# A four-layer decoder kernel: cross attention in row quarters and halves with a fourth buffer, one subtraction moved to GpSimd, and other counts of unread products at the norms

## The chip, the cores and the metric

The kernel runs on one core of a Trainium2 chip, as one program. The metric is device time in microseconds of one execution, lower is better. TensorE does the matrix products (the profile shows its weight loads apart, as PEld), VectorE (DVE), ScalarE (ACT) and GpSimd (POOL) the elementwise work, and SyncE (SP) issues the transfers. A matrix product reads a moving operand of up to 512 columns from SBUF, against weights loaded before, and writes to one of eight PSUM banks.

## The reference

Twelve stages run one after another over x, two sequences (B = 2) of 512 tokens of width 128: four layers of self attention, cross attention and feed forward. Each adds to x what it computes from a norm of x. The change is in two kinds of cross attention, and at the norms. Cut to those, in numpy's manner:

```
# l0x: 16 heads of 64, context of 77 rows of width 96 and one null key (78 keys), a key mask
q = norm(x) * g @ Wq ; k, v = context @ Wkv            # 16 heads of 64 columns
s = q_h @ k_h.T / 8, masked                            # (512, 78) per head and sequence
x = x + norm(concat_h(softmax(s) @ v_h) @ Wout) * g_out
# l2x, l3x ("narrow"): 16 heads of 8 inside a width of 128, 77 keys
q = norm(x) @ Wq + bq ; k = context @ Wk + bk ; v = context @ Wv + bv
s = q_h @ k_h.T / sqrt(8)                              # l2x: clipped to +-10000 before its softmax
x = x + concat_h(softmax(s) @ v_h) @ Wo + bo
```

## The kernel before

The program is written by hand: every engine has its own list of instructions, in the order in which the code below issues them, and the engines meet at counting semaphores (`then_inc` raises one, `wait_ge` waits for it). Nothing is scheduled or reordered by a planner; `plan` only gives the items of work their PSUM banks. x stays in SBUF throughout. The stages are called l0a, l0x, l0f, l1a, ... l3f (a self attention, x cross attention, f feed forward).

**A cross attention loop** is one of 16 steps. In l0x, l2x and l3x a step is eight heads (`half`) of one tile of 128 query tokens (`qt`, NQ = 4) of one sequence (`b`). A step's work goes round the engines:

- TensorE (`cross_tensor`): the scores of eight heads into two banks (`a.scores`), 128 x 616 or 128 x 624 numbers. At L816 two heads of 64 rows share one product of 128 rows, since `keys_own` holds zeros in the other head's rows; in the narrow stages (L1615) `keys_own` holds all 128 rows for each of the 16 heads, with a head's own eight rows kept and the others zero.
- VectorE (`cross_vector`): in l2x a clip from PSUM to SBUF (L709), then the maxima (L711), the subtraction of them (L712), and for the step before the sums of the exponentials (L717) and their reciprocals (L720).
- ScalarE (`cross_scalar`): the exponential (L731), and the copy of the turned probabilities of two steps back out of PSUM (L738).
- GpSimd (`cross_gpsimd`): the probabilities, exponentials times reciprocals (L748).
- TensorE again: eight transposes of the probabilities of step k - 2 (L686), and the values of step k - 6: two heads a step. In l0x (L827) they are of 64 columns each, and VectorE copies them out (L894). In the narrow stages (L1623) `values_own` holds for each head 128 columns, zero but for the head's own eight, and all sixteen heads add up in one bank, over 512 tokens at a time.

The probabilities `m.xp` have three buffers (k % 3), so the first instruction of VectorE's step k waits until step k - 3 is transposed.

**At every norm** VectorE takes moments of four tiles at a time (`half_moments`, L133 to L143, which raises `var_ready`), GpSimd the power -1/2 (L184), VectorE scales the tiles (L158), TensorE transposes them (L209) and ScalarE copies them out (L217). Meanwhile TensorE runs products of the identity whose result nobody reads (`keep_busy`, L193): `first` of them, then `second` after the second half's variance. `turned` waits for ScalarE's copies before the projections.

**At the start** `consts` are loaded in one queue by SyncE (L3026), and every other engine waits for all of them; among them are `rows8` and `cols8`, by which the narrow stages make `keys_own` (L1674) and `values_own` (L1712).

## Time and profile before

| | us |
|---|---|
| median of 3 runs | 1818.76 (1816.85 to 1821.48) |
| the profiled execution | 1830.47 |
| its span, first to last instruction | 1828.6 |
| TensorE busy in it | 1582.6 |
| VectorE busy | 1039.3 |
| ScalarE busy | 678.5 |
| GpSimd busy | 376.1 |
| mean granted TensorE clock | 0.907 of full |

The profiled execution is 11.7 us longer than the median of the others. Times in the rows below are of this one. "x8" in a row is a count of instructions; a matrix product of 32-bit numbers shows as two records (one product of 512 columns as x2), a transpose as one. `[0.78 <-PE psum L819]` is idle time of the engine before the row, and what ended it. A granted clock of 1.00 is 2.4 GHz, 0.50 is 1.2 GHz.

### The profile page before, as it was taken

Reading aid. Unit: us, or ns where it says so; the run is one execution under the profiler, and the core shown is the slowest. Engines: PE = TensorE matmul, PEld = TensorE weight load, DVE = VectorE, ACT = ScalarE, POOL = GpSimd, SP = SyncE. Lnnn points to the kernel's source line nnn. Section 1 sums busy time; section 2 is a strip of 40 time slices with the busy share of each in tenths; the row PEclk is TensorE's granted clock in tenths of the full one; section 3 lists DMA queues with packets and bytes.
Section 4 is the critical chain, followed back from the end, with each engine's and each line's share of the span. In section 5 each row is a group of like instructions: output and inputs, shape, how many; then the busy total and the mean of one; then the engine's idle time right before and its main releaser. Section 6 shows DMA issues by size and latency. Waiting matters only on the chain. (4 is left out here: it accounts for less than half of the span.)

```text
span 1828.6 us, 24507 instructions
## 1 busy us (share of the span) xinstructions
PE 1582.6 (87%) x9019; PEld 953.6 (52%) x9027; DVE 1039.3 (57%) x1963; ACT 678.5 (37%) x1652; POOL 376.1 (21%) x366
## 2 busy tenths in 40 slices
PE   6999899999999989968988848836989988899996
PEld 3665446445555565554567535522435555564444
DVE  4676574334554555567392366489875554465665
ACT  3774331333555534423102134213555555460001
POOL 3000120001000000033011034255764433410000
PEclk8999999998787889989687979977999999899999
DMA  3000002210000000000104000000111100100000
GB/s 128 2 2 4 1 1 102 97 46 13 1 1 1 1 14 8 9 3 0 60 1 156 9 29 39 20 15 24 35 35 18 18 13 14 17 7 24 23 23 12
DMA packets 14075, 46.92 MB, mean 26 GB/s; under 512 B 3032, under 2 KB 4870, under 8 KB 13328
## 3 DMA queue, kind: packets, MB, share of 16 engines
q1 hardware_dynamic: 13968, 45.49, 8.1%
q8 instruction: 68, 1.11, 0.3%
q14 instruction: 39, 0.32, 0.1%
HBM read 40.73 MB, written 0.56 MB: 23 GB/s over the span
## 5 line engine op out<-in xcount | busy, mean ns | idle before, releaser
L503 DVE TENSOR_REDUCE quad_max<-psum 128x1 f32<-128x128 f32 (+3 forms) x256 | 113.6, 486 | 116.2 <-PE psum L399 115.9
L184 POOL TENSOR_TENSOR rstd<-var,minus_half 128x4 f32<-128x4 f32 x30 | 30.6, 1022 | 655.2 <-DVE var L143 585.5
L468 ACT ACTIVATE pt<-psum,quad_max 128x128 f32<-128x128 f32 (+3 forms) x256 | 133.5, 525 | 83.0 <-DVE quad_max L503 80.5
L193 PE MATMUL psum<-ident 128*128 128x128 f32 x960 | 124.4, 293 | 45.0 <-DVE wide L2069 20.9
L2433 PE MATMUL psum<-slots,xn_t 128*128 128x512 f32 x256 | 113.8, 606 | 42.1 <-DVE pt L2606 42.1
L193 PEld LDWEIGHTS psum<-ident 128*128 128x128 f32 x960 | 120.6, 208 | 49.3 <-DVE wide L2069 21.5
L2469 PE MATMUL psum<-pt,slots 128*128 128x512 f32 x256 | 129.8, 594 | 2.1 <-DVE pt L2619 1.9
L2619 DVE TENSOR_TENSOR pt<-psum,wide 128x512 f32<-128x512 f32 x128 | 87.8, 691 | 52.9 <-PE psum L2462 43.8
L2303 DVE TENSOR_REDUCE duo_max<-psum 128x1 f32<-128x512 f32 x128 | 82.3, 686 | 56.4 <-PE psum L2204 55.3
L415 PE MATMUL psum<-ident,pt 128*128 128x128 f32 x640 | 99.9, 306 | 12.0 <-DVE wide L1212 10.8
L2433 PEld LDWEIGHTS psum<-slots,xn_t 128*128 128x128 f32 x256 | 48.1, 193 | 107.6 <-DVE pt L2606 52.6
L2278 ACT ACTIVATE p<-psum,duo_max 128x512 f32<-128x512 f32 x128 | 86.8, 683 | 46.7 <-DVE duo_max L2303 41.5
L2519 ACT ACTIVATE pt<-psum,p 128x64 f32<-128x64 f32 x256 | 58.0, 393 | 101.4 <-POOL wide L2673 51.0
L775 ACT ACTIVATE o_t<-psum 128x512 f32<-128x512 f32 x20 | 11.7, 595 | 216.4 <-PE psum L567 145.9
L415 PEld LDWEIGHTS psum<-ident,pt 128*128 128x128 f32 x640 | 81.7, 160 | 17.5 <-DVE wide L1212 12.3
L748 POOL TENSOR_TENSOR p<-p,xrsum 128x616 f32<-128x616 f32 (+1 forms) x48 | 58.6, 1222 | 146.3 <-DVE xrsum L720 146.3
L1090 DVE TENSOR_TENSOR p<-p,wide 128x512 f32<-128x512 f32 x64 | 44.1, 692 | 76.8 <-ACT p L1037 66.8
L2218 PE MATMUL psum<-ident,p 128*128 128x128 f32 x512 | 70.5, 279 | 18.9 <-DVE wide L2328 18.9
L2263 DVE COPY pt<-psum 128x512 f32<-128x512 f32 x64 | 44.2, 691 | 72.5 <-PE psum L2218 72.5
L686 PE MATMUL psum<-ident,p 128*77 128x128 f32 (+1 forms) x384 | 58.2, 300 | 29.5 <-POOL p L748 29.1
L2238 PEld LDWEIGHTS psum<-pt,wide 128*64 128x64 f32 x1024 | 58.2, 143 | 48.9 <-issue 20.0
L2204 PE MATMUL psum<-heads 64*128 64x512 f32 x256 | 75.5, 669 | 6.3 <-POOL heads L2350 6.3
(451 smaller groups left out, 3181.1 us busy)
## 6 DMA issues: line engine op xcount, KB each, us to landing
slots<-in_s_l2f SPq DMA_DIRECT2D x8, 578.0 KB, 3.8
keys_own<-in_s_l2f SPq DMA_DIRECT2D x8, 578.0 KB, 5.6
slots<-in_s_l0f SPq DMA_DIRECT2D x8, 514.0 KB, 3.6
wide<-scratch_gates SPq DMA_DIRECT2D x8, 512.0 KB, 7.6
slots<-in_s_l3v SPq DMA_DIRECT2D x8, 512.0 KB, 3.7
slots<-in_s_l3o SPq DMA_DIRECT2D x8, 512.0 KB, 3.6
weights<-in_w_l1a SPq DMA_DIRECT2D x1, 2624.0 KB, 9.1
weights<-in_w_l0x SPq DMA_DIRECT2D x1, 2113.0 KB, 10.7
```

The lines of the kernel that those rows point to most:

```text
L193: nc.tensor.matmul(m.ps[bank][:, 0:P], m.ident[:, :], m.ident[:, :], start=True, stop=True, skip_group_check=True)
L415: last = nc.tensor.transpose(bank[:, g * P:(g + 1) * P], m.quad_p[:, n % 2, g, kt * P:(kt + 1) * P], m.ident[:, :])
L468: nc.scalar.activation(m.quad_p[:, i % 2, g, 0:keys], m.ps[g][:, 0:keys], ACT.Exp, bias=m.quad_max[:, i % 2, g:g + 1], accum_out=sum_colum ...
L503: nc.vector.tensor_reduce(m.quad_max[:, n % 2, g:g + 1], m.ps[g][:, 0:keys], AX.X, ALU.max, negate=True).then_inc(m.quad_negmax, 1)
L748: nc.gpsimd.tensor_tensor(pr, pr, m.xrsum[:, k % 2, :].rearrange("p (h o) -> p h o", o=1).broadcast_to([P, 8, nk]), ALU.mult).then_inc(m.p ...
L2204: nc.tensor.matmul(m.ps[2 * (n % 2) + e], m.pair_rope[own, r % 2, 0, b * S + qt * P:b * S + (qt + 1) * P], m.pair_rope[own, r % 2, 1, b * ...
L2218: last = nc.tensor.transpose(bank[:, kt * P:(kt + 1) * P], m.p[:, 2 * (n % 2) + e, kt * P:(kt + 1) * P], m.ident[:, :])
L2278: nc.scalar.activation(m.p[:, 2 * (i % 2) + e, :], m.ps[2 * (i % 2) + e], ACT.Exp, bias=m.duo_max[:, i % 2, e:e + 1], accum_out=m.duo_sum[ ...
L2303: nc.vector.tensor_reduce(m.duo_max[:, n % 2, e:e + 1], m.ps[2 * (n % 2) + e], AX.X, ALU.max, negate=True).then_inc(m.duo_negmax, 1)
L2433: nc.tensor.matmul(m.ps[n % MIX_BANKS], m.xn_t[:, t * P:(t + 1) * P], m.slots[:, pair % 2, h * S:(h + 1) * S], start=True, stop=True).then ...
L2469: nc.tensor.matmul(m.ps[6 + b], m.slots[:, s, e * P:(e + 1) * P], m.gated[:, q % 4, :], start=False, stop=False, skip_group_check=True).th ...
L2619: tt(m.gated[:, k % 4, :], m.ps[k % 4], out, ALU.mult).then_inc(m.spread_gated, 1)
```

## The change

1. **Score products by rows.** In l0x each head's 64 rows are a product of their own (eight of 78 columns a step, even heads in one bank and odd ones in the other, in turn), and the mask's product comes first. In l2x and l3x `keys_own` has 32-row quarters: a product covers four heads on 32 rows, and a step has two such products, on two quarters, in two banks.
2. **Value products by columns in l2x and l3x.** A head's `values_own` has the 32 columns of its quarter; each product writes 32 partitions of the bank, for the 128 tokens of one tile. They come after every second step, 16 at a time; for that the steps go tile by tile with `half` innermost (`narrow_units`).
3. **Four buffers** for the probabilities, and the transposes of step k - 3 instead of k - 2 in TensorE's order.
4. **l2x:** VectorE keeps the clip and the maxima, GpSimd subtracts (L761 of the new file), and VectorE's sums are of step k - 2.
5. **l0x:** ScalarE copies the values out, and `context_v`; the norm stands first in VectorE's order.
6. **Unread products.** `busy_through_norm` has a third group, `turned` adds four in each of its 14 calls, other groups stand in the second and third step of a cross loop, two before the transposes of each narrow step.
7. **`rows8` and `cols8`** are no longer loaded.

The diff, cut to its core (other callers of `busy_through_norm` change their counts only: l0f 13, 16 to 12, 6, 12 and 12, 8 to 14, 6; l1f, l2a, l3a and the first of l3f 12, 8 to 12, 6; l2f 12, 8 to 12, 8, 10; the second of l3f 12, 16 to 14, 6, 10; where no third count stands it is 4):

```diff
-def busy_through_norm(nc, pe, m, norm, first, second):
+def busy_through_norm(nc, pe, m, norm, first, second, third=4):
+
     keep_busy(nc, m, first)
     pe.wait_ge(m.var_ready, 2 * norm)
     keep_busy(nc, m, second)
+    pe.wait_ge(m.rstd_ready, 2 * norm - 1)
+    keep_busy(nc, m, third)
...
-def turned(m, pe, name):
+def turned(nc, m, pe, name):
+    keep_busy(nc, m, 4)
...
-    for k in range(XSTEPS + 6):
+    for k in range(XSTEPS + 3 + NQ):
         if k < XSTEPS:
             b, half, qt = units[k]
             wait(pe, m.negmax_ready, a.s0 + k - 1)
-            for j in range(2):
-                last = a.scores(m.ps[2 * (k % 2) + j], b, half, j, qt)
-            last.then_inc(m.scores_ready, 1)
-        j = k - 2
+            a.scores([m.ps[2 * (k % 2) + e] for e in range(2)], b, half, qt).then_inc(m.scores_ready, 1)
+            if k in (1, 2):
+                keep_busy(nc, m, (14, 4)[k - 1], 7)
+        j = k - 3
...
-    for k in range(XSTEPS + 1):
+    lag = 2 if a.clip else 1
+    for k in range(XSTEPS + lag):
...
             if a.clip:
                 m.dve.done(nc.vector.tensor_scalar(to, scores, a.clip, -a.clip, ALU.min, ALU.max))
-                scores = to
-            m.dve.done(nc.vector.tensor_reduce(m.xmax[:, k % 2, :].rearrange("p (g h) -> p g h", g=2), scores, AX.X, ALU.max))
-            nc.vector.tensor_tensor(to, scores, spread(m.xmax[:, k % 2, :]), ALU.subtract).then_inc(m.negmax_ready, 1)
-        j = k - 1
+                wait(dve, m.negmax_ready, a.s0 + k - 1)
+                nc.vector.tensor_reduce(largest, to, AX.X, ALU.max).then_inc(m.xmax_ready, 1)
+            else:
+                m.dve.done(nc.vector.tensor_reduce(largest, scores, AX.X, ALU.max))
+                nc.vector.tensor_tensor(to, scores, spread(m.xmax[:, k % 2, :]), ALU.subtract).then_inc(m.negmax_ready, 1)
+        j = k - lag
...
-    for k in range(XSTEPS):
-        pool.wait_ge(m.rsum_ready, a.s0 + k + 1)
-        pr = m.xp[:, k % 3, 0:8 * nk].rearrange("p (h k) -> p h k", k=nk)
-        nc.gpsimd.tensor_tensor(pr, pr, m.xrsum[:, k % 2, :].rearrange("p (h o) -> p h o", o=1).broadcast_to([P, 8, nk]),
-                                ALU.mult).then_inc(m.probs_ready, 1)
+    heads = lambda k: m.xp[:, k % XP_BUFFERS, 0:8 * nk].rearrange("p (h k) -> p h k", k=nk)
+    each = lambda ap: ap.rearrange("p (h o) -> p h o", o=1).broadcast_to([P, 8, nk])
+    lag = 2 if a.clip else 0
+    for k in range(XSTEPS + lag):
+        if a.clip and k < XSTEPS:
+            pool.wait_ge(m.xmax_ready, k + 1)
+            nc.gpsimd.tensor_tensor(heads(k), heads(k), each(m.xmax[:, k % 2, :]), ALU.subtract).then_inc(m.negmax_ready, 1)
+        j = k - lag
+        if j >= 0:
+            pool.wait_ge(m.rsum_ready, a.s0 + j + 1)
+            nc.gpsimd.tensor_tensor(heads(j), heads(j), each(m.xrsum[:, j % 2, :]), ALU.mult).then_inc(m.probs_ready, 1)
...
+    def scores(banks, b, half, qt):
+        for e in range(2):
+            nc.tensor.matmul(banks[e][:, 0:4 * nk], m.ones_bf[0:1, :], m.mask_row[0:1, b, :], start=True, stop=False,
                              skip_group_check=True)
-        return nc.tensor.matmul(bank[:, 0:4 * nk], m.ones_bf[0:1, :], m.mask_row[0:1, b, :], start=False, stop=True,
-                                skip_group_check=True)
+        for i in range(4):
+            g = 4 * half + i
+            for e in range(2):
+                rows = slice(64 * e, 64 * e + 64)
+                last = nc.tensor.matmul(banks[e][:, i * nk:(i + 1) * nk], m.wide[rows, g, b * S + qt * P:b * S + (qt + 1) * P],
+                                        m.keys_own[rows, b, g * nk:(g + 1) * nk], start=False, stop=i == 3,
+                                        skip_group_check=True)
+        return last
...
+        units = narrow_units()
+        own = lambda g: slice(32 * g, 32 * g + 32)
+        for k in range(XSTEPS + 5):
+            if k < XSTEPS:
+                b, half, qt = units[k]
+                if clip:
+                    wait(pe, m.xmax_ready, k - 1)
+                else:
+                    wait(pe, m.negmax_ready, a.s0 + k - 1)
+                for x in range(2):
+                    rows = own(2 * half + x)
+                    last = nc.tensor.matmul(m.ps[2 * (k % 2) + x][:, 0:GROUP * SC], m.q_t[rows, b * S + qt * P:b * S + (qt + 1) * P],
+                                            m.keys_own[rows, b, 0:GROUP * SC], start=True, stop=True)
+                last.then_inc(m.scores_ready, 1)
+                if k in (1, 2):
+                    keep_busy(nc, m, (16, 4)[k - 1], 7)
+            n = k - 3
+            if 0 <= n < XSTEPS:
+                pe.wait_ge(m.probs_ready, a.s0 + n + 1)
+                wait(pe, m.cross_taken, a.x0 + n)
+                keep_busy(nc, m, 2, 4)
+                for h in range(8):
+                    last = nc.tensor.transpose(m.ps[4 + h // 4][0:SC, (h % 4) * P:(h % 4 + 1) * P],
+                                               m.xp[:, n % XP_BUFFERS, h * SC:(h + 1) * SC], m.ident[:, :])
+                last.then_inc(m.turned_ready, 1)
+            n = k - 5
+            if n >= 0 and n % 2 == 1:
+                b, _, qt = units[n]
+                pe.wait_ge(m.cross_taken, a.x0 + n + 1)
+                if n == 1:
+                    pe.wait_ge(m.narrow_values, a.v0 // 2 + 1)
+                bank = fill(m, pe, f"{stage}o{b}") if qt == 0 else m.ps[6 + b]
+                for j in range(GROUP):
+                    for g in range(GROUP):
+                        last = nc.tensor.matmul(bank[own(g), qt * P:(qt + 1) * P], m.values_own[0:SC, b, g, j, :],
+                                                m.xpt[0:SC, g // 2, g % 2 * GROUP + j, qt * P:(qt + 1) * P],
+                                                start=qt == 0 and j == 0, stop=qt == NQ - 1 and j == GROUP - 1,
+                                                skip_group_check=True)
+                last.then_inc(m.pv_done if qt < NQ - 1 else filled(m, f"{stage}o{b}"), 1)
```

**The order of TensorE in l0x**, in the second half of the loop, before: `keys_own,wide` are the scores, `mask_row,ones_bf` the mask, `ident,p` the transposes, `pt,context_v` the values.

```order
L827 MATMUL psum<-pt,context_v 64x512 x2
L816 MATMUL psum<-keys_own,wide 128x156 x2
L819 MATMUL psum<-mask_row,ones_bf 128x312
L816 MATMUL psum<-keys_own,wide 128x156 x2
L819 MATMUL psum<-mask_row,ones_bf 128x312
L686 MATMUL psum<-ident,p 78x128 x8
```

The same place after:

```order
L847 MATMUL psum<-pt,context_v 64x512 x2
L831 MATMUL psum<-mask_row,ones_bf 128x312 x2
L837 MATMUL psum<-keys_own,wide 128x78 x8
L691 MATMUL psum<-ident,p 78x128 x8
L847 MATMUL psum<-pt,context_v 64x512 x2
```

Two masks now stand together ahead of eight narrower score products; the transposes are those of the step before the ones they were.

**The order of TensorE at the end of l2x's loop**, before: `keys_own,q_t` are the scores, `pt,heads` the values.

```order
L1615 MATMUL psum<-keys_own,q_t 128x308 x2
L686 MATMUL psum<-ident,p 77x128 x8
L1623 MATMUL psum<-pt,heads 128x512 x2
L686 MATMUL psum<-ident,p 77x128 x8
L1623 MATMUL psum<-pt,heads 128x512 x2
L686 MATMUL psum<-ident,p 77x128 x8
L1623 MATMUL psum<-pt,heads 128x512 x10
```

After:

```order
L1643 MATMUL psum<-keys_own,q_t 128x308 x2
L193 MATMUL psum<-ident 128x128 x2
L1654 MATMUL psum<-ident,p 77x128 x8
L193 MATMUL psum<-ident 128x128 x2
L1654 MATMUL psum<-ident,p 77x128 x8
L1666 MATMUL psum<-pt,heads 32x128 x16
L193 MATMUL psum<-ident 128x128 x2
L1654 MATMUL psum<-ident,p 77x128 x8
L193 MATMUL psum<-ident 128x128 x2
L1654 MATMUL psum<-ident,p 77x128 x8
L1666 MATMUL psum<-pt,heads 32x128 x32
```

Fourteen value products of 512 columns stood behind the last scores' transposes; now 48 of 128 columns do, each of 32 columns of weights.

**The order of VectorE in l2x's loop**, one step, before and then after:

```order
L709 TENSOR_SCALAR p<-psum 128x616
L711 TENSOR_REDUCE xmax<-p 128x8
L712 TENSOR_TENSOR p<-p,xmax 128x616
L717 TENSOR_REDUCE xsum<-p 128x8
L720 RECIPROCAL xrsum<-xsum 128x8
```

```order
L716 TENSOR_SCALAR p<-psum 128x616
L718 TENSOR_REDUCE xmax<-p 128x8
L726 TENSOR_REDUCE xsum<-p 128x8
L729 RECIPROCAL xrsum<-xsum 128x8
L716 TENSOR_SCALAR p<-psum 128x616
```

The subtraction left VectorE, and the sums behind it belong to a step one earlier than they did.

## Rows read from the trace of the kernel before

**Rows 1.** The page's costliest groups: busy, mean ns of one, idle before.

```profile
L748 POOL TENSOR_TENSOR p<-p,xrsum 128x616 f32<-128x616 f32 (+1 forms) x48 | 58.6, 1222 | 146.3 <-DVE xrsum L720 146.3
```

**Rows 2.** Busy time by stretch: length, each engine's busy us, granted clock, DMA.

```profile
229.00:261.00 32.00, 31.75 (x178) 18.52 (x178) 24.68 (x41) 13.05 (x16) 9.84 (x8) 1.00 0.00 1
...
825.00:866.50 41.50, 35.99 (x155) 21.57 (x153) 31.22 (x49) 15.56 (x20) 10.95 (x9) 1.00 0.00 0
866.50:892.60 26.10, 24.77 (x45) 12.27 (x45) 1.67 (x4) 3.78 (x5) 2.44 (x2) 0.52 0.00 0
...
1105.30:1115.00 9.70, 6.49 (x22) 4.46 (x21) 6.50 (x11) 3.17 (x4) 6.32 (x3) 0.74 0.00 0
1115.00:1125.50 10.50, 7.60 (x41) 5.69 (x40) 8.99 (x15) 4.88 (x6) 3.65 (x3) 0.92 0.01 2
1125.50:1162.50 37.00, 35.70 (x153) 21.40 (x151) 23.30 (x39) 15.40 (x20) 10.95 (x9) 1.00 0.00 1
1162.50:1180.30 17.80, 15.76 (x41) 8.08 (x40) 0.99 (x3) 3.97 (x5) 2.39 (x2) 0.81 0.00 0
```

**Rows 3.** Timeline of one l0x step: start, us, instruction, idle before.

```profile
239.93 1.07 PE L686 MATMUL psum<-ident,p 128*78 128x128 f32 x8
...
240.93 1.08 PE L827 MATMUL psum<-pt,context_v 78*64 78x512 f32 x4
...
241.94 0.80 PE L816 MATMUL psum<-keys_own,wide 128*128 128x156 f32 x4
...
242.41 0.64 DVE L894 COPY wide<-psum 128x512 f32<-128x512 f32 x1
...
243.96 0.81 DVE L711 TENSOR_REDUCE xmax<-psum 128x8 f32<-128x624 f32 x1 [0.91 <-PE psum L819]
```

**Rows 4.** Timeline of two l2x steps.

```profile
841.88 1.10 PE L686 MATMUL psum<-ident,p 128*77 128x128 f32 x8 [1.16 <-POOL p L748]
842.42 0.80 DVE L712 TENSOR_TENSOR p<-p,xmax 128x616 f32<-128x616 f32 x1
...
842.82 1.88 PE L1623 MATMUL psum<-pt,heads 77*128 77x512 f32 x4
...
844.54 1.20 PE L1615 MATMUL psum<-keys_own,q_t 128*128 128x308 f32 x4
...
850.53 1.10 PE L686 MATMUL psum<-ident,p 128*77 128x128 f32 x8 [1.16 <-POOL p L748]
```

**Rows 5.** Timeline of the values behind the loops of l2x and l3x.

```profile
874.73 17.27 PE L1623 MATMUL psum<-pt,heads 77*128 77x512 f32 x20
...
1170.41 9.21 PE L1623 MATMUL psum<-pt,heads 77*128 77x512 f32 x20
```

**Rows 6.** Timeline of products on 32 rows or columns in l0a.

```profile
56.18 1.08 PE L430 MATMUL psum<-pt,wide 128*32 128x128 f32 x32
57.19 0.91 PE L397 MATMUL psum<-k_t,heads 32*128 32x384 f32 x4
58.03 0.28 PE L399 MATMUL psum<-future,ident_bf 128*128 128x128 bf16 x2
```

**Rows 7.** Timeline of weight loads on 32 rows (l0a) and 128 rows (l0x).

```profile
57.19 0.30 PEld L397 LDWEIGHTS psum<-k_t,heads 32*128 32x128 f32 x4 [0.20 <-issue]
...
201.84 0.56 PEld L816 LDWEIGHTS psum<-keys_own,wide 128*128 128x128 f32 x4
```

**Rows 8.** Timeline of the first step of l2x.

```profile
793.60 9.90 POOL L1712 TENSOR_TENSOR heads<-context_v,cols 77x2048 f32<-77x2048 f32 x2 [4.26 <-DVE context_v L1680]
...
801.33 2.82 DVE L712 TENSOR_TENSOR p<-p,xmax 128x616 f32<-128x616 f32 x1
```

**Rows 9.** Timeline of TensorE at l1f's norm.

```profile
751.62 2.05 PE L193 MATMUL psum<-ident 128*128 128x128 f32 x16 [0.88 <-DVE var L143]
```

**Rows 10.** DMA issues: KB each.

```profile
cols<-in_cols SPq DMA_DIRECT2D x1, 1088.0 KB
```

**Rows 11.** Busy time of a stretch at the start; the last column is GB/s.

```profile
10.00:15.00 5.00, 0.77 (x3) 0.78 (x4) 0.79 (x4) 0.79 (x3) 0.77 (x3) 1.00 1.04 395
```

More of the change, by code:

```diff
@@ L662 @@
 XSTEPS = 2 * B * NQ
+XP_BUFFERS = 4
 def cross_units():
@@ L857, in l0_cross_scalar, with take_values @@
                              scale=64 ** -0.5).then_inc(emptied(m, f"l0xq{2 * g}"), 1)
-    a.unit_done = lambda eng, b, half: read(m, eng, f"l0xo{(b * 2 + half) * 4 + 3}")
+    a.unit_done = lambda eng, b, half, qt: read(m, eng, f"l0xo{(b * 2 + half) * 4 + 3}") if qt == 0 else None
+    def take_values(n):
+        b, half, i = cross_units()[n]
+        bank = read(m, act, f"l0xo{n}")
+        nc.scalar.activation(m.wide[:, 4 * half + i, b * S:(b + 1) * S], bank[:, :], ACT.Copy).then_inc(emptied(m, f"l0xo{n}"), 1)
+    first = NQ + 3
+    a.scalar_after = {first + n: take_values for n in range(XSTEPS + 2 - first)}
     cross_scalar(nc, act, m, a)
+    for n in range(XSTEPS + 2 - first, XSTEPS):
+        take_values(n)
     copy_out_scalar(nc, act, m, "l0xy", m.y_t)
@@ L878, in l0_cross_vector @@
                               [1, B, 4, SC])).then_inc(m.cross_ready, 1)
-    for n in range(2 * B):
-        b, j = divmod(n, 2)
-        bank = read(m, dve, f"l0xv{n}")
-        nc.vector.tensor_copy(m.context_v[0:SC, b, j * S:(j + 1) * S],
-                              bank[0:SC, :]).then_inc(emptied(m, f"l0xv{n}"), 1)
-    norm_to_turn(nc, dve, m, twice=True)
     for g in range(NPAIR):
@@ L1577, in l2_attn_vector, with narrow_units @@
     add_to_x(nc, dve, m, "l2ay")
+def narrow_units():
+    return [(b, half, qt) for b in range(B) for qt in range(NQ) for half in range(2)]
 def narrow_cross(stage, clip=None):
@@ L1611, in tensor @@
         pe.wait_ge(m.narrow_keys, a.v0 // 2 + 1)
-        def scores(bank, b, half, j, qt):
-            at = (8 * half + 4 * j) * SC
-            return nc.tensor.matmul(bank[:, 0:4 * SC], m.q_t[:, b * S + qt * P:b * S + (qt + 1) * P],
-                                    m.keys_own[:, b, at:at + 4 * SC], start=True, stop=True)
-        def values(pe, b, half, i):
-            if i == 0:
-                pe.wait_ge(m.narrow_values, a.v0 // 2 + 1)
-            bank = fill(m, pe, f"{stage}o{b}") if half == 0 and i == 0 else m.ps[6 + b]
-            for h in (2 * i, 2 * i + 1):
-                last = nc.tensor.matmul(bank, m.values_own[0:SC, b, 8 * half + h, :], m.xpt[0:SC, half, h, :],
-                                        start=half == 0 and h == 0, stop=half == 1 and h == 7, skip_group_check=True)
-            if i == 3:
-                last.then_inc(filled(m, f"{stage}o{b}") if half else m.pv_done, 1)
```

145 lines of the change are left out of this document (66 added, 79 removed).

## The prediction

> **What bounds the kernel now.** I read the page first: TensorE is busy most of the span and its mean granted clock is below full, so the questions are which stages it bounds and where it runs at half clock. Then the busy time by stretch through the three cross loops, then the timeline of one step of each, then the rows just before a product or an operation that the change alters.
>
> In the second half of l0x's loop TensorE is busy for 31.75 of 32.00 us at full clock, while GpSimd does 8 multiplications: 4.0 us a step, and TensorE is the bound; VectorE is busy for 24.7 [rows 2]. The step's parts follow without a gap: transposes 1.00 us (from 239.93 to 240.93), values 1.01, scores and mask about 1.95, and VectorE waits for the mask [rows 3].
>
> In l2x two steps take 8.65 us (841.88 to 850.53), so 4.32 each. Here nobody is full: transposes wait 1.16 us for GpSimd's multiplication of step k - 2, values are another 1.7 us in front of the next scores (842.82 to 844.54), and scores 1.0 [rows 4]. The loop is a ring: VectorE, ScalarE, VectorE, GpSimd, TensorE, with the transposes of step k - 2 queued on TensorE ahead of scores that VectorE waits for. In the whole stretch TensorE is busy for 36.0 of 41.5 us, VectorE for 31.2 [rows 2].
>
> Behind the loop comes a tail: 26.1 us in l2x, 17.8 in l3x, nearly all TensorE's values, in l2x at a granted 0.52 [rows 2]. The last ten value products (20 records) took 17.27 us at 1.2 GHz in l2x and 9.21 at 2.4 GHz in l3x [rows 5]. Nothing lies beside it.
>
> **The change part by part.**
>
> *Narrow steps (l2x, l3x), TensorE.* Scores: two products on 32 rows each, 308 columns, in different quarters. In l0a two such products of 384 columns on two quarters (4 records) start at 57.19 and the next product starts at 58.03, 0.84 us; one after the other they would be 4 x 768 / 2.4 GHz = 1.28. They ran as one pair, 0.64, with 0.20 on top [rows 6]. So 308 columns cost 0.51 + 0.20 = 0.71, for 1.0 now. Values: in l0a 32 records of 32 columns of weights and 128 moving columns took 1.01 us (56.18 to 57.19) [rows 6]; a pair of steps now has just that, 0.51 a step for 1.7. Transposes stay, 0.94 (841.88 to 842.82) [rows 4]. The two unread products: 16 records are 2.05 us less the last one's own latency, 0.118 a record [rows 9], so 0.47. Sum 2.63.
>
> *Narrow steps, the others.* In l2x VectorE had five instructions of which four are 0.80 us (the subtraction at 842.42 for one) [rows 4]; without the subtraction it has 0.84 + 0.82 + 0.82 + 0.12, about 2.6 with the sequence's gaps. GpSimd gets a second pass of the same shape, and 1.222 us is its mean now [rows 1]: 2.44, and 2.6 if each starts a little late. In l3x VectorE keeps its 2.5. Four buffers and transposes a step later take the ring out of the way: clip, maximum, subtraction, exponential, sum, multiplication and transposes are 0.8 + 0.8 + 1.2 + 0.7 + 1.0 + 1.2 + 1.0 = 6.7 us, over four steps at 2.7 there is room for it. I take 2.75 us a step in both: three engines at 2.6 each seldom meet without loss. The bounds are 2.6 (no loss) and 3.2 (0.2 us for each of three changes of product form).
>
> *l2x.* From the first subtraction, 801.33, to the end of the loop, 866.5, fifteen steps take 65.2 us [rows 8, 2]; at 2.75 they take 41.3: -24. The first subtraction is among it, at 2.82 us for the usual 0.80: it stood until GpSimd's `values_own` (9.90 us for two instructions from 793.60) was through [rows 8]. The new `values_own` has a quarter of the columns, and the subtraction isn't VectorE's. The tail goes from 26.1 us [rows 2] to one multiplication 1.2, transposes 1 to 2, their copy 1.0, sixteen products 1.0 to 2.0, the copy of the output 0.6, and the lagging sums: 8. That is -18. The unit of work that made it, ten to fourteen whole-width products behind the last scores, is now spread over the loop, where it hides at 0.51 a step. l2x: -42.
>
> *l3x.* Its sixteen steps are 9.7 + 10.5 + 37.0 = 57.2 us [rows 2]; at 2.75 they are 44: -13. Tail 17.8 to about 6: -12. l3x: -25.
>
> *Before both loops.* The transposes of xn waited for VectorE's `keys_own` and `context_v`; `values_own` starts at 793.60 because they end there [rows 8]. With 308 columns for 1232 they end some 1.8 us earlier, and the norm's 20 unread products behind the variance are ten: -3.5 for the two.
>
> *l0x.* TensorE's step keeps 2.0 of transposes and values. Scores: two masks of 312 columns in one pass at 2.4 GHz, 0.26; 16 records of 78 columns are set by their weight loads. Four loads on 128 rows took 0.56 us, four on 32 rows in two quarters 0.30 [rows 7]: 0.12 each one after the other, and two at a time where rows differ. The order alternates between the two halves, so 8 x 0.12 = 0.96, and 0.2 for the change of form: 1.4, step 3.4. The other end is every load by itself, 16 x 0.12 + 0.46 = 2.4, step 4.4. I take 3.4, since rows 6 and 7 both show pairs. 16 x 0.6 = -10. VectorE gives up 0.64 us of copies a step [rows 3]: worth nothing while TensorE is the bound, and ScalarE takes it at 40% load (13.05 of 32.00) [rows 2]. If that cover went, VectorE would be next at about 3.2. The 14 unread products after the second step's scores are 28 x 0.118 = 3.3 us in which the third step's scores stand behind them; they fill a wait of about that length. l0x: -10.
>
> *Start.* `cols8` is 1.088 MB [rows 10] in a queue that moved 395 GB/s, and TensorE starts at 14.2 (busy for 0.77 of the five us to 15.0) [rows 11]: -2.8, call it -3. Nothing hides it.
>
> *Norms.* Behind the variance there are 3 more products in l0a, 2 in each of l0f, l1f, l2a, l3a and l3f's first, 4 in l1x, 10 in l2f: 27 x 0.236 = 6.4 us [rows 9], and TensorE's transposes stand behind them. The four in `turned` (0.95 us) lie beside ScalarE's two copies. The third group's wait is for the first half's root, which is through when the second variance is. Below: 0, where VectorE is later anyway; I take +6.5.
>
> *Clock.* The narrow loops will have a stretch or two at half clock, as before (0.74 granted in l3x's first 9.7 us [rows 2]), and now cost more there, since TensorE is no longer waiting: +5.
>
> Sum: -42 - 25 - 3.5 - 10 - 3 + 6.5 + 5 = -72. The profiled execution would go from 1830.5 to 1758; it stands 11.7 above the median of the runs, so from 1818.8 the median goes to **1747**.
>
> **Against a rule of the skill.** Weight loads on few rows went two at a time in rows 7. The Trainium skill (TensorE: Matmul & The Clock Gate, section on LDWEIGHTS) says that a load's time goes by its columns, so that 32 x 128 takes what 128 x 128 does, though it also lets loads of different row groups overlap. By the first alone l0x's step is the 4.4 above; by the row it is 3.4. And the Trainium skill (TensorEngine Tiling (Array Packing), Key Properties) has TensorE drained at each change of tiling mode; the trace agrees with 0.20 us beside a pair [rows 6], and by it three changes a step are what makes 3.2 of 2.6 in the narrow loops.
>
> **The rivals.**
>
> *A. As above*: 1747, with 1728 to 1765 for steps of 2.6 to 3.0 us. Chance 0.55.
>
> *B. Weight loads and changes of form cost in full*: l0x at 4.4 a step is +16 against the sum, narrow steps at 3.2 are +14: 1777; one of the two alone 1763. For it: each step changes form three times, more than l0a does. Against: rows 7. Chance 0.12.
>
> *C. Half clock through the narrow loops.* TensorE's step there would be 1.23 + 1.9 + 1.0 + 0.95, some 4.9 to 5.0 us, +34 a stage: 1811; for half of the steps 1780. For it: in l2x's tail TensorE was busy for 24.8 of 26.1 us and was granted 0.52 all the while, with products on 77 rows [rows 2], and the new ones fill less of the array. Against: the loop before them, with the same products and idle time between, was granted 1.00. Chance 0.15.
>
> *D. GpSimd and VectorE shut each other out in l2x.* The subtraction on VectorE stood 2.0 us until GpSimd's instruction ended [rows 8]. If VectorE's reductions from SBUF did so too, the step would be up to 2.6 + 2.4 = 5.0, +36: 1783. Against: GpSimd multiplied 1.222 on average with VectorE going on [rows 1]. Chance 0.03. The Trainium skill (Perfetto Trace Analysis, Optimizing Scalar/DVE Operations) warns that the two share a read port and that moving work between them might not help; row 801.33 is that, for an operation with two operands in SBUF, and none is left in the loop.
>
> *E. The fillers also hold the clock elsewhere.* The mean granted clock of 0.907 is some 170 us with half of their work lost; if the attention stages behind the norms lose fewer stretches, 15 to 30 us more go: 1725. Chance 0.11.
>
> *F. Slower.* TensorE at 1.2 GHz through all three loops, l0x's too: its step of 3.4 becomes 6.7, +53 on top of C: 1864. It decides from about 59% of all 48 steps at half clock (72 of 122 us). Against: l0x's loop is granted 1.00 with TensorE 99% busy [rows 2]. Chance 0.04.
>
> **How the numbers follow.** About 0.3% (5.5 us) is what a measurement of this kernel tells from no change. A, B, D and E are faster, and of C all but its full case near 1811, which I give 0.02 of "same": faster 0.94, same 0.02, slower 0.04. The range reaches from 1722 to 1790: it takes in A, B, D, most of E, and the half of C; outside are C in full, the best of E and F, some 0.16.
>
> **What would show it.** Right: multiplications 2.7 to 2.9 us apart in l2x and l3x, 3.4 in l0x; value records of 32 columns, 32 in about 1.1 us; less than 9 us from the last sums to the output's copy in l2x; TensorE's first product near 11.3; transposes at l1f's norm 0.47 us later against its variance; GpSimd's new subtraction at 1.22 and VectorE's reductions still at 0.80 beside it. Wrong: a granted clock well below 0.9 in the narrow loops, score records of l0x 0.12 us apart, VectorE's rows over 1 us, or ScalarE late with the values' copies, so that TensorE waits for a bank.

## The result and the profile after

The changed kernel took 1766.2 us (median of 4 runs, 1763.8 to 1769.3), the kernel before 1820.1 on the same chip (4 runs): ratio 0.969, 95% interval 0.966 to 0.971, some 54 us less. In a second set of runs, with the experiments below, it was 1766.8 against 1819.7, ratio 0.971 (0.968 to 0.974). The forecast was 1747, its range 1722 to 1790. The profiled execution took 1765.7 us with a span of 1763.9.

Engines and TensorE's granted clock, from the page of the changed kernel:

```profile
PE 1547.0 (88%) x9939; PEld 963.0 (55%) x9939; DVE 1006.2 (57%) x1926; ACT 686.2 (39%) x1664; POOL 383.1 (22%) x394
...
PEclk8999999998787899999896979959999999999999
```

TensorE is busy for 88% of a span that is 65 us shorter (87% before), and for 36 us less in all, so what went was not only waiting but its own work. Busy time by stretch in the changed kernel: l2x's loop, l2x's tail, l3x's loop (columns as in [rows 2]):

```profile
785.80:838.00 52.20, 39.47 (x388) 29.41 (x392) 34.60 (x58) 22.77 (x28) 34.61 (x30) 0.92 0.00 1
838.00:849.30 11.30, 10.10 (x121) 8.52 (x109) 0.00 (x0) 3.61 (x5) 0.04 (x1) 0.59 0.01 2
...
1065.30:1108.40 43.10, 38.32 (x423) 28.82 (x422) 35.15 (x58) 22.85 (x28) 19.45 (x16) 1.00 0.00 1
```

Behind the length, a line has the busy us (and records) of TensorE, its weight loads, VectorE, ScalarE and GpSimd, then granted clock, DMA share and GB/s. The two loops compute the same but for the clip, and l2x takes 9 us more: TensorE is busy for 39.5 of 52.2 us there, for 38.3 of 43.1 in l3x, and its clock is below full in one and full in the other. In both, GpSimd and VectorE have time left (34.6 of 52.2 us each in l2x).

One step of l0x with values in it, timeline of the changed kernel (beside [rows 3]):

```profile
226.12 0.43 PE L831 MATMUL psum<-mask_row,ones_bf 1*128 1x312 bf16 x2
...
226.48 1.12 PE L837 MATMUL psum<-keys_own,wide 64*128 64x78 f32 x16
...
226.90 1.23 POOL L765 TENSOR_TENSOR p<-p,xrsum 128x624 f32<-128x624 f32 x1 [2.20 <-DVE xrsum L729]
...
227.53 1.07 PE L691 MATMUL psum<-ident,p 128*78 128x128 f32 x8
...
228.53 1.08 PE L847 MATMUL psum<-pt,context_v 78*64 78x512 f32 x4
...
229.54 0.43 PE L831 MATMUL psum<-mask_row,ones_bf 1*128 1x312 bf16 x2
...
230.32 1.23 POOL L765 TENSOR_TENSOR p<-p,xrsum 128x624 f32<-128x624 f32 x1 [2.20 <-DVE xrsum L729]
```

3.42 us from mask to mask and between multiplications, where 3.4 was forecast. Eight score products on alternate halves (16 records) take 1.12 us.

Two steps of l2x, timeline of the changed kernel (beside [rows 4]):

```profile
788.57 0.79 PE L1643 MATMUL psum<-keys_own,q_t 32*128 32x308 f32 x4
...
789.41 0.80 DVE L716 TENSOR_SCALAR p<-psum 128x616 f32<-128x616 f32 x1 [1.49 <-PE psum L1643]
...
790.24 0.80 DVE L718 TENSOR_REDUCE xmax<-p 128x8 f32<-128x616 f32 x1
...
791.12 1.22 POOL L761 TENSOR_TENSOR p<-p,xmax 128x616 f32<-128x616 f32 x1 [1.67 <-DVE xmax L718]
...
792.29 1.22 POOL L765 TENSOR_TENSOR p<-p,xrsum 128x616 f32<-128x616 f32 x1
...
793.56 0.71 PE L193 MATMUL psum<-ident 128*128 128x128 f32 x4 [1.44 <-POOL p L765]
...
794.11 1.04 PE L1654 MATMUL psum<-ident,p 128*77 128x128 f32 x8
...
795.07 0.79 PE L1643 MATMUL psum<-keys_own,q_t 32*128 32x308 f32 x4
```

Read it as a chain: scores of step k, clip 0.84 us later, maximum 0.83, subtraction 0.88, then on the same engine the multiplication of step k - 2 at 1.17, the unread products at 1.27, its transposes 0.55, and the scores of step k + 2 0.96 later, since on TensorE they stand behind these transposes. The sum is 6.50 us for two steps, 3.25 for one: a ring of two steps, for which nobody is busy all the time. These steps have no values in them yet. A few steps later the same ring has them as well:

```profile
806.35 0.79 PE L1643 MATMUL psum<-keys_own,q_t 32*128 32x308 f32 x4
...
812.86 1.08 PE L1666 MATMUL psum<-pt,heads 77*32 77x128 f32 x32
813.87 0.79 PE L1643 MATMUL psum<-keys_own,q_t 32*128 32x308 f32 x4
```

Between the transposes and the next scores now stand the 32 records of values, 1.01 us, and the ring takes 7.52 us, 3.76 a step, at full clock.

Where the time went, by the starts of GpSimd's operation on the variances, one or two at every norm (us; the second pair is one more profiled execution of each kernel, among the experiments below):

| part | forecast | first pair | second pair |
|---|---|---|---|
| start | -3 | -3.3 | -1.5 |
| l0a | +0.7 | +0.5 | +1.0 |
| l0x and its norm | -10 | -11.7 | -14.7 |
| l0f, l1a | +0.5 | -6.1 | -4.4 |
| l1x, l1f, l2a | +1.9 | +1.8 | +4.1 |
| l2x | -43.8 | -25.0 | -14.1 |
| l2f, l3a | +2.8 | +2.0 | +1.5 |
| l3x | -26.8 | -23.0 | -19.1 |
| l3f to the end | +0.5 | +0.1 | -2.0 |
| clock, not placed | +5 | | |
| sum | -72 | -64.7 | -49.3 |

The forecast's 6.5 for norms is shared out here by the number of products, its 3.5 before both loops halved between l2x and l3x. The last column's sum is of unrounded values.

### The profile page after: what moved, and what is told of

The parts are those of the page before. It is cut to its first block and busy times, and to the rows that moved or that the text cites. A ratio compares the mean times of both kernels' runs of the same rounds, so it can differ in the third digit from the quotient of the medians.

```text
span 1763.9 us, 26362 instructions
## 1 busy us (share of the span) xinstructions
PE 1547.0 (88%) x9939; PEld 963.0 (55%) x9939; DVE 1006.2 (57%) x1926; ACT 686.2 (39%) x1664; POOL 383.1 (22%) x394
## 5 line engine op out<-in xcount | busy, mean ns | idle before, releaser
L193 PE MATMUL psum<-ident 128*128 128x128 f32 x1360 | 179.8, 289 | 61.8 <-DVE wide L2111 20.9
L193 PEld LDWEIGHTS psum<-ident 128*128 128x128 f32 x1360 | 168.1, 202 | 81.0 <-DVE wide L2111 21.5
L2345 DVE TENSOR_REDUCE duo_max<-psum 128x1 f32<-128x512 f32 x128 | 82.4, 685 | 56.3 <-PE psum L2246 55.1
L2320 ACT ACTIVATE p<-psum,duo_max 128x512 f32<-128x512 f32 x128 | 86.7, 682 | 45.4 <-DVE duo_max L2345 40.5
L419 PEld LDWEIGHTS psum<-ident,pt 128*128 128x128 f32 x640 | 81.9, 160 | 17.5 <-DVE wide L1225 12.3
L791 ACT ACTIVATE o_t<-psum 128x512 f32<-128x512 f32 x20 | 11.7, 595 | 190.2 <-PE psum L571 145.9
L2260 PEld LDWEIGHTS psum<-ident,p 128*128 128x128 f32 x512 | 58.4, 143 | 40.6 <-DVE wide L2370 20.3
L765 POOL TENSOR_TENSOR p<-p,xrsum 128x616 f32<-128x616 f32 (+1 forms) x48 | 58.5, 1221 | 92.0 <-DVE xrsum L729 92.0
```

Source lines behind the costliest of these rows:

```text
L193: nc.tensor.matmul(m.ps[bank][:, 0:P], m.ident[:, :], m.ident[:, :], start=True, stop=True, skip_group_check=True)
L419: last = nc.tensor.transpose(bank[:, g * P:(g + 1) * P], m.quad_p[:, n % 2, g, kt * P:(kt + 1) * P], m.ident[:, :])
L2260: last = nc.tensor.transpose(bank[:, kt * P:(kt + 1) * P], m.p[:, 2 * (n % 2) + e, kt * P:(kt + 1) * P], m.ident[:, :])
L2320: nc.scalar.activation(m.p[:, 2 * (i % 2) + e, :], m.ps[2 * (i % 2) + e], ACT.Exp, bias=m.duo_max[:, i % 2, e:e + 1], accum_out=m.duo_sum[ ...
L2345: nc.vector.tensor_reduce(m.duo_max[:, n % 2, e:e + 1], m.ps[2 * (n % 2) + e], AX.X, ALU.max, negate=True).then_inc(m.duo_negmax, 1)
```

## The experiments

All but the two repeats are edits of the changed kernel. Three sets of four shared a chip and the runs of the kernel before, whose medians were 1819.7, 1823.9 and 1819.7: first the changed kernel again, the nearer multiplication, the subtraction on VectorE and no fillers at the start; then the kernel before again, the norms, the steps without fillers and the halves in turn; then the rest. Between sets the ratios are what to compare; they come from the single runs and need not be the quotient of the two medians (for the 1748.5 below that would be 0.961, not 0.956). A filler is a product that nobody reads. Of every cross loop the table gives the time from the start of its first to the end of its last multiplication by GpSimd, and for l2x also the stretch ahead of it (from the norm's second variance) and behind it (to the next norm's first).

| kernel | median, ratio to before (95%) | l0x | l2x: ahead, loop, behind | l3x |
|---|---|---|---|---|
| before | 1820.1, 1 | 57.9 | 19.2, 61.5, 31.1 | 55.6 |
| before again | 1809.4 (one run) | 57.7 | 19.2, 61.4, 20.1 | 55.1 |
| changed | 1766.2, 0.969 | 48.6 | 16.3, 52.3, 18.2 | 43.1 |
| changed again | 1766.8, 0.971 (0.968 to 0.974) | 47.0 | 16.3, 52.2, 18.2 | 43.1 |
| multiplication a step nearer | 1750.8, 0.961 (0.959 to 0.964) | 47.0 | 13.8, 43.4, 13.5 | 43.1 |
| subtraction on VectorE | 1757.9, 0.966 (0.963 to 0.969) | 47.0 | 14.8, 48.4, 13.0 | 43.1 |
| no fillers at the loops' start | 1775.3, 0.974 (0.972 to 0.977) | 52.1 | 15.0, 61.6, 15.8 | 46.6 |
| norms' fillers as before | 1772.0, 0.972 (0.970 to 0.974) | 47.0 | 17.4, 58.5, 17.5 | 43.1 |
| no fillers in the steps | 1770.1, 0.971 (0.968 to 0.974) | 48.6 | 16.3, 61.3, 18.5 | 37.5 |
| l0x halves in turn | 1776.1, 0.976 (0.973 to 0.979) | 54.2 | 16.3, 59.3, 14.2 | 43.1 |
| three buffers | 1853.1, 1.018 (1.012 to 1.023) | 54.4 | 16.3, 119.0, 16.0 | 52.4 |
| nearer, l3x without fillers | 1748.5, 0.956 (0.950 to 0.963) | 48.6 | 13.8, 43.4, 13.5 | 37.5 |
| nearer, no fillers in steps | 1749.2, 0.960 (0.954 to 0.965) | 48.6 | 13.8, 47.5, 11.8 | 37.5 |
| nearer, l3x without fillers, fewer at start | 1744.2, 0.956 (0.951 to 0.961) | 47.3 | 13.8, 43.4, 13.5 | 39.2 |

**Both kernels again.**

> The changed kernel itself once more, so that the others of this call stand beside it on one chip. Both theories expect a ratio of 0.969 to the kernel before, and l2x from its first subtraction to the end of its last multiplication in some 58 us (53 us for the fifteen steps between first and last subtraction).

> The kernel before in another profiled execution, which shows how much of the 11.7 us between its first profiled execution and its median lies in one place. Theory 1 (TensorE's clock differs from execution to execution in stages that the change does not touch): span 1812 to 1822, and the differences lie in stretches with another granted clock. Theory 2 (the profiler adds them everywhere): again 1828, the landmarks the same.

The changed kernel repeats itself: 52.2 us in l2x's loop again. The kernel before does not: the second profiled execution spans 1807.6 us, 21 less, and 11 of them lie in one place, behind l2x's loop. Busy time there, in the first trace of the kernel before and in the second:

```profile
869.00:892.10 23.10, 23.10 (x39) 10.62 (x38) 0.00 (x0) 2.58 (x4) 0.00 (x0) 0.50 0.00 0
```

```profile
863.50:878.50 15.00, 13.56 (x43) 6.99 (x41) 1.13 (x5) 3.12 (x4) 0.00 (x0) 0.93 0.00 0
```

The same products at 1.2 GHz in one and nearly all at 2.4 in the other. The forecast took the first for the rule. How often either comes is not known: the eleven runs of the kernel before in the last set reach from 1811 to 1835 us.

**The multiplication a step nearer** (GpSimd and VectorE, l2x alone):

```
 cross_vector:   -    lag = 2 if a.clip else 1
                 +    lag = 1
 cross_gpsimd:   -    lag = 2 if a.clip else 0
                 +    lag = 1 if a.clip else 0
```

> Only in l2x: GpSimd multiplies step k - 1 behind the subtraction of step k (the changed kernel: step k - 2), and VectorE sums one step later than the maximum for two. Theory 1 (the two-step ring: scores, clip, maximum, subtraction k, multiplication k - 2, transposes k - 2, scores k + 2, 6.5 us for two steps): with the multiplication one step nearer the ring spans three steps and falls away; the step goes from 3.25 to 3.54 down to the 3.0 that l3x has, so 7 to 8 us less in the fifteen steps, and a total of about 1758. Theory 2 (GpSimd, now with two passes, or TensorE at half clock is what holds l2x): nothing within 2 us, and VectorE now waits for the exponential besides, up to 3 us more.

The loop went from 52.2 to 43.4 us, l2x in all from 86.7 to 70.7, and the total by 16. Theory 1 holds, and the step comes out as said: in the later steps the multiplications are 2.44 and 3.56 us apart in turn, 3.0 on average, just as in l3x. The loop's 8.8 us are what was expected of it; another 2.5 come ahead of it (the first multiplication is issued one step earlier) and 4.7 behind it, where the loop's last products run at a granted 1.00 for 0.59. Busy time of its loop, and two steps of its timeline:

```profile
783.20:826.60 43.40, 38.20 (x424) 28.84 (x423) 35.27 (x60) 24.50 (x29) 35.87 (x30) 1.00 0.01 2
```

```profile
805.25 0.68 PE L193 MATMUL psum<-ident 128*128 128x128 f32 x4 [0.48 <-ACT pt L745]
805.47 1.21 POOL L765 TENSOR_TENSOR p<-p,xrsum 128x616 f32<-128x616 f32 x1
...
806.74 1.22 POOL L761 TENSOR_TENSOR p<-p,xmax 128x616 f32<-128x616 f32 x1
...
807.91 1.21 POOL L765 TENSOR_TENSOR p<-p,xrsum 128x616 f32<-128x616 f32 x1
...
808.47 0.71 PE L193 MATMUL psum<-ident 128*128 128x128 f32 x4
```

TensorE no longer waits for POOL L765 (13.4 us in the changed kernel's loop, none here); GpSimd now works without a gap at places, at 35.9 of 43.4 us. What the ring costs apart from the clock can be read from the first ten steps, first in the changed kernel and then here:

```profile
785.80:820.00 34.20, 24.70 (x250) 18.47 (x251) 24.28 (x40) 15.64 (x19) 23.85 (x21) 1.00 0.00 1
```

```profile
783.20:811.50 28.30, 24.98 (x253) 18.39 (x252) 24.43 (x41) 15.82 (x19) 23.93 (x21) 1.00 0.01 1
```

Both at full clock and with the same work, 5.9 us apart: 0.6 us a step are the ring's, two thirds of the loop's gain. The other 2.9 us come in the steps behind, where the changed kernel was granted 0.78.

**The subtraction back on VectorE**, four buffers kept:

In outline:

```
 cross_vector:   -  clip; max -> xmax_ready              (lag 2)
                 +  clip; max; subtract -> negmax_ready  (lag 1)
 cross_gpsimd:   -  subtract k, multiply k - 2
                 +  multiply k
```

> Only in l2x: the maxima are subtracted by VectorE again, as in the kernel before, with four buffers and the transposes a step later kept. Theory 1 (the ring through GpSimd limits): VectorE's 0.84 + 0.82 + 0.82 + 0.82 + 0.12 = 3.4 us a step take over, 51 us for the fifteen steps where the changed kernel has 53: the subtraction on GpSimd brought nothing, the total is the changed kernel's within 3 us. Theory 2 (moving the subtraction is what made l2x shorter): the step goes back towards 4.3, fifteen steps to 60 or more, the total to 1775.

Every gap between multiplications but the last is 3.28 or 3.29 us, VectorE's five instructions; busy time of its loop:

```profile
785.70:834.10 48.40, 38.23 (x422) 28.57 (x419) 46.14 (x74) 22.75 (x28) 19.46 (x16) 1.00 0.01 1
```

VectorE is the bound (46.1 of 48.4), and yet l2x takes 76.2 us for the changed kernel's 86.7, the total 1758 for 1767. Theory 2 falls, and theory 1 was too cautious (9 us less where it said within 3): moved as the change moves it, the subtraction on GpSimd costs 10 us in l2x, by its ring and by the clock together; only with the multiplication a step nearer does it gain.

**Three buffers, transposes a step earlier**, in outline:

```
-XP_BUFFERS = 4
+XP_BUFFERS = 3
 transposes of step  - k - 3   + k - 2    (values a step earlier too)
```

> The changed kernel with three buffers for the scores and the transposes of step k - 2, as before the change, and the values a step earlier with them; all else stays. Theory 1 (in l2x the ring runs through the multiplication of step k - 2, which stands on GpSimd behind the subtraction of step k; with transposes k - 2 it closes after one step): a step of l2x is scores 0.84, clip 0.83, maximum 0.88, subtraction 1.17, multiplication 1.27, unread products 0.44, transposes 1.07 and half of the values' 1.0, 7.0 us at full clock, so its loop goes from 52 to 100 us or more; l3x and l0x, where that ring spans three steps and has 8 us in it, stay within 2 us: total 1815 or more. Theory 2 (GpSimd's 2.44 us a step or the clock sets l2x's pace): l2x's loop at most 10 us longer.

```profile
819.54 0.80 DVE L718 TENSOR_REDUCE xmax<-p 128x8 f32<-128x616 f32 x1
...
820.42 1.22 POOL L761 TENSOR_TENSOR p<-p,xmax 128x616 f32<-128x616 f32 x1 [5.80 <-DVE xmax L718]
...
821.59 1.22 POOL L765 TENSOR_TENSOR p<-p,xrsum 128x616 f32<-128x616 f32 x1
...
822.86 1.22 PE L193 MATMUL psum<-ident 128*128 128x128 f32 x4 [4.20 <-POOL p L765]
...
827.59 1.40 PE L1643 MATMUL psum<-keys_own,q_t 32*128 32x308 f32 x4
...
829.03 0.80 DVE L716 TENSOR_SCALAR p<-psum 128x616 f32<-128x616 f32 x1 [7.75 <-PE psum L1643]
```

With the same instructions l2x's loop takes 119.0 us: the ring closes after one step, and VectorE stands 7.75 us. That is theory 1: 7.85 us a step at a granted 0.57, where it said 7.0 at full clock, and no engine but TensorE (63.1 us, at about half clock) is busy for a third of it. Its second half was a miss: l3x is 9.3 us longer and l0x 5.8 to 7.4 in the loop, where I expected 2. There the transposes wait for a multiplication of the step just done, so the fourth buffer with the later transposes is worth some 15 us in those two loops as well.

**Fillers ahead of the transposes left out** (`keep_busy(nc, m, 2, 4)` in l2x and l3x), alone and with the nearer multiplication, in l3x or in both:

> The two unread products ahead of each step's transposes in l2x and l3x are left out. Theory 1 (they are on the path at 0.44 us each pair: TensorE bounds l3x with 6.0 us for two steps, and they are a member of l2x's ring): l3x goes to VectorE's 2.6 us a step, 5 to 6 us less, l2x 3 us less, total 8 to 9 us less. Theory 2 (they keep the clock): at least one more stretch at half clock in each of the two loops, total 0 to 15 us more.

> The multiplication in l2x one step nearer, as in the run that did that alone, and in l3x alone the two unread products ahead of each step's transposes left out. Theory 1 (what the single runs showed adds up: l2x 16 us less, l3x 7.5 us less): total 7 us below the run with the nearer multiplication, some 1743. Theory 2 (the clock behind l3x depends on its products): l3f and its sampling lose 3 us or more, total 1746 to 1752.

> The multiplication in l2x one step nearer, and the two unread products ahead of the transposes left out in l2x and l3x both. Theory 1 (the half clock in l2x came because TensorE stood in the ring, and falls away with it, as in l3x without these products): l2x's step goes to about 2.5 us, another 7 us less there, total 1736. Theory 2 (these products are what keeps l2x's clock, whatever the ring): a stretch of half clock in l2x, its loop 50 us or more, total 1750 to 1755.

Busy time of l2x's loop and then of l3x's without them; and, from the last of the three, l2x's:

```profile
789.50:850.70 61.20, 52.94 (x328) 35.90 (x332) 34.83 (x58) 22.88 (x28) 34.59 (x30) 0.51 0.00 1
...
1076.50:1114.00 37.50, 32.47 (x374) 22.75 (x372) 34.38 (x58) 24.20 (x28) 19.36 (x16) 1.00 0.00 1
```

```profile
786.60:834.10 47.50, 42.61 (x370) 29.47 (x369) 35.60 (x60) 24.16 (x30) 35.83 (x30) 0.75 0.00 1
```

In l3x they only cost: 2.45 us a step without them, VectorE's pace, 5.6 us less in the loop and 7.5 in all, at full clock. In l2x the clock was lower without them: 0.51, and still 0.75 with the ring out of the way, where theory 1 of that run had expected full. So each theory is right in one loop. These are one trace each, and the clock of l2x's loop also moves by itself while the ring is there: in the halves-in-turn run, whose edit lies in l0x alone, the loop took 59.3 us at a granted 0.74. But the order holds in all of them: with the ring 0.67 to 0.92 with these fillers and 0.51 without, with the nearer multiplication 1.00 in three traces with them and 0.75 without. The totals of the three runs with the nearer multiplication overlap with each other; that l3x is 7.5 us shorter shows in the trace alone. Behind l3x nothing was lost for it (638.8 us from its norm to the end with l3x bare, 641.3 with its fillers), so theory 2 of that run does not hold, though its median, 1748.5, is the one that theory named.

**Fillers at the start of the loops**, none, and fewer:

```
-            if k in (1, 2):
-                keep_busy(nc, m, (14, 4)[k - 1], 7)     # 16 and 4 in l2x, l3x; 8 in l1x
```

> The unread products behind the second and third step's scores of the cross loops are left out (14 and 4 in l0x, 8 in l1x, 16 and 4 in l2x and in l3x). Theory 1 (they stand before the third step's scores, which the wait they fill does not cover): the third scores start 4 to 5 us earlier in l0x and about 2 us earlier in l2x and l3x, total 6 to 9 us less. Theory 2 (they hold the clock): the granted clock falls in the first ten us of the loops, and the total is 0 to 10 us more.

> As the run with the nearer multiplication and l3x bare, and the unread products behind the second step's scores cut from 14 to 8 in l0x and from 16 to 10 in l2x and l3x (those behind the third stay at 4). Theory 1 (they need only fill the wait for the first probabilities, and what is left keeps the clock): the third step's scores start 1.4 us earlier in each loop, where VectorE waits for them, total 2 to 4 us less than that run. Theory 2 (fewer let the clock fall, as with none): 5 us more or worse, with 4.4 us between l0x's first multiplications.

Theory 1 was right on the first gap only: l0x's first two multiplications are 2.82 us apart where the changed kernel has 4.60 to 6.20. But the clock was at half from there on, where the changed kernel was granted 0.99, and from the third to the sixth they are 4.4 apart:

```profile
200.00:220.00 20.00, 19.66 (x134) 14.63 (x132) 14.11 (x22) 7.06 (x9) 6.14 (x5) 0.54 0.01 2
```

The total is 8.4 us more (theory 2); the profiled execution, 1785.9, was the longest of its six, so its rows show the bad side. With 8 and 10 of them nothing is to be told from 14 and 16: 1744.2 beside 1748.5, with intervals that overlap.

**The norms' fillers as before** (no third group, none in `turned`, the old counts):

> The changed kernel with the unread products of the norms as they were before: no third group behind the first root, none between the transposes of xn and the wait for their copies, the counts of before. By the prediction's term 27 products behind the variances go, 6.5 us less. Theory 1 (the transposes of xn wait for VectorE anyway and the products pay themselves back by the clock of l0f and l1a, whose stretches were 3.5 and 2.6 us shorter in the changed kernel's trace): 0 to 8 us more, with lower granted clock behind the norms. The rival, that the products cost what they last: 4 to 7 us less.

By the ratios 0.972 against 0.971, which tells nothing. By the trace both theories are seen: 0.45 us less at l1f's norm and 0.45 at l2a's, as the term said, but 1.1 to 2.8 us more ahead of l0x's loop, and l2x's loop at 58.5. l0f and l1a together were 4.4 us shorter than in the changed kernel's first trace, so the third group is not what shortened them.

**l0x's scores, one half after the other:**

```
-        for i in range(4):
-            for e in range(2):
+        for e in range(2):
+            for i in range(4):
```

> l0x's eight score products of a step in another order: all four on the lower 64 rows, then all four on the upper, where the changed kernel alternates. Theory 1 (two weight loads on different rows go at the same time, which is why 16 records take 1.12 us): the records take 1.9 us, the step 4.2 for 3.43, 16 steps 11 to 13 us more. Theory 2 (a load of 78 columns by 64 rows is as fast alone, and the order means nothing): within 2 us of the changed kernel.

The products of this run, and the weight loads of a step in the changed kernel and in this run:

```profile
231.43 1.63 PE L837 MATMUL psum<-keys_own,wide 64*128 64x78 f32 x16
```

```profile
229.91 0.97 PEld L837 LDWEIGHTS psum<-keys_own,wide 64*128 64x128 f32 x16 [0.26 <-issue]
```

```profile
231.42 1.48 PEld L837 LDWEIGHTS psum<-keys_own,wide 64*128 64x128 f32 x16 [0.26 <-issue]
```

1.63 us for the 1.12 of the changed kernel, 3.93 between multiplications for 3.43, the loop 5.6 to 7.2 us longer. The order does matter; it is worth 0.5 us a step, where I expected 0.8. Each half also writes its own PSUM bank, so the order alternates the banks too, and the two are not told apart by the totals. The single load records show the overlap itself: in both runs the loads of one half start 0.11 us after each other, and in the changed kernel a load of each half starts within 0.01 us of one of the other. Where the four of one half end and those of the other begin, this run's loads overlap too, which fits that it lost less than expected. The Trainium skill (TensorE: Matmul & The Clock Gate, section on LDWEIGHTS) states that a load's time goes by its columns and not by its rows; the trace agrees, with 0.11 us for 64 rows here and 0.12 for 128 rows in [rows 7]. It is not by itself the 4.4 us step of rival B, since two halves load at once.

## Why the prediction was right and where it was not

**Right.** TensorE's first product at 10.96 us (11.3 said); l0x at 3.42 to 3.43 us a step (3.4), its stage 12 to 15 us shorter (10); the value records of 32 columns, 32 in 1.08 us; the narrow scores; the two engines do not shut each other out (POOL L761 1.22 us, VectorE's reductions 0.80), so D is out. l3x: 3.0 us a step with values in it, 2.79 over the loop (2.75), and 43.1 us where 44 were said. B is out too: l0x has no 4.4 us step, and l3x without fillers goes at VectorE's 2.45, so its changes of form don't cost 3.2; F is out by the sign. 1766.2 lies in the range, but 1 us outside the 1728 to 1765 of A, the rival that was held for the likeliest. At the norm of [rows 9] the fillers last 2.50 us for 2.05, and the transposes stand 0.45 later; that row is l2a's norm, not l1f's as it is called in [rows 9] and in the prediction; l1f's fillers, at 706.74, last 2.50 as well. The row after, of l2a's norm:

```profile
732.37 2.50 PE L193 MATMUL psum<-ident 128*128 128x128 f32 x20 [0.88 <-DVE var L143]
```

**Wrong: the step of l2x's loop.** The prediction wrote that four buffers and transposes a step later "take the ring out of the way", 6.7 us over four steps. It added up the chain of one step's own scores and left out the order on GpSimd, where the multiplication of step k - 2 stands behind the subtraction of step k. So the ring spans two steps, not four: at full clock 3.25 us a step without values and 3.76 with them, where 2.75 were taken; over the loop 3.40, single gaps between 2.44 and 6.89. From first to last multiplication the loop went from 61.5 to 52.3, not by the 24 us of the forecast. That was seen in three ways: one step more in the ring (the nearer multiplication) took it away and gave 5.9 us in ten steps with the clock full on both sides, one less (three buffers) made the loop 119 us, and the subtraction's return to VectorE did better than the change.

**Wrong: the clock in l2x.** TensorE, busy for 39.5 of 52.2 us, was granted 0.92 in the loop and 0.59 in the tail, in both traces of the changed kernel. The forecast allowed 5 us for such stretches, over both loops. Rival C, half clock, came here in part. With the ring gone the same products ran at 1.00 from end to end, 2.9 us less in the loop's last third and 4.7 behind it, the latter in part because one step fewer is left to finish there.

**Wrong: the tail's -18, and how the profile was carried over to the median.** The 26.1 us of [rows 2] were an execution at half clock; the second trace has 20.1 us behind the loop (to the next norm) for 31.1. The forecast booked these 11 us as gain, and then took off 11.7 us once more because the profiled execution stood above the median: 1758 became 1747. The new tail was longer than the 8 us of the forecast: from the last sums (835.25) to the output's copy (848.71) it is 13.5 us, where less than 9 was the sign of being right. The excess and the tail may well be the same 11 us; two traces can't show it, since the second lies as far below the median as the first above it. But the subtraction needed the changed kernel's profiled execution to be long by as much, and it was not (1765.7 beside a median of 1766.2). Against that execution the forecast was off by 8 us (1758 for 1765.7), against the median by 19. Measured with the kernel before at its better tail, l2x brought 14 us and not 44. That the total still fell in the range owes something to luck: l2x was 19 to 30 us short, and l0x with its norm, l0f and l1a together brought 8 to 10 us more than forecast, the larger part of it from stretches that hardly changed.

**Sizes.** l3x was 23.0 and 19.1 for 26.8: its tail fell by 8.1, from 24.6 to 16.6, for the 12 said. Its step of 3.0 with values is TensorE's own, 2.76 (2.63 said), and 0.48 in every second step for ScalarE's copy (the wait on ACT L745, as at 805.25 above), which the sum had at nothing. l0x brought 2 to 5 more. l0f and l1a were 4 to 6 us shorter with nothing changed in them but a few products; in the traces of the experiments they lie from 4.4 below the changed kernel's to 5.6 above. That spread goes with the clock (l1a took 204.4 us at a granted 0.83 in the norms' run and 214.0 at 0.78 in the run without start fillers, against 208.5 at 0.81 in the changed kernel), and rival E can be neither shown nor ruled out by it.

**Open.** Why l2x loses its clock without the fillers while l3x does not, with the same TensorE instructions and both at 2.45 us a step at first, was not settled. Nor was why the ring and the lower clock come together. What narrower score and value products brought by themselves was not measured either: no run takes them back.

## What to carry to other kernels

When an operation moves to another engine, write down that engine's new order and follow one result through all the queues until it closes on itself; divide by the number of steps it spans. If the span is two where the plan says four, look at the lag on that engine first: here one step less was worth 16 us, for two numbers in the code, while the move without it cost 10 us in its stage. Before a long stretch at half clock is booked as gain, look whether another execution of the same kernel has it, and never subtract the profile's excess over the median from a forecast that already removes the place where the excess may lie. The version with the nearer multiplication beats both kernels, with l3x's fillers (1750.8 us, 0.961 of the kernel before, 0.959 to 0.964) or without (1748.5, 0.956, 0.950 to 0.963).

## What the runs showed of the hardware

The same unread products (two ahead of the transposes) go with a granted 1.00 in one loop, 0.75 without, and only cost 0.37 us a step in its twin (43.1 for 37.5 us, both at 1.00). And the same products, in the same kernel, behind the same loop, ran at a granted 0.50 in one execution and 0.93 in the next, 11 us apart. An edit in l0x alone left l2x's loop at 59.3 us and 0.74 for 52.2 and 0.92. Two products on different 64-row halves in turn save 0.06 us a product over four on one half and four on the other, since 16 records take 1.12 us and not 1.63; the weight loads of the two halves start together, those of one half 0.11 us apart.
